# A convolution, attention and mixture block in one kernel: residual and normalisation moved ahead, attention reordered, the convolution's first column split off

## The chip, the cores and the metric

The kernel runs on one core of one Trainium2 chip. The metric is the device time of one execution in microseconds; the runs before the change had a median of 121.98 us (three runs, 121.91 to 122.46). The profile is of one execution whose own time was 122.06 us; its instructions span 120.3 us. The 1.76 us between the two lie outside the instructions.

## The reference

Eight images of 64 channels and 16 x 16 pixels, all in float32. What is computed, cut to what matters:

```python
x = x + conv_ref(ln_c(x), ...)             # ln_c: over the 64 channels, eps 1e-6
t = to_tokens(x)                           # 8 x 256 pixels, 64 channels each
t = t + ffn_ref(ln_t(t), ...)              # ln_t: over the 64 channels, eps 1e-5
...
# conv_ref
qkv = einsum('bchw,oc->bohw', x, w_qkv)    # 192 channels
dw = conv_5x5_depthwise(qkv, w_dw)
pw = einsum('bgihw,goi->bgohw', dw, w_pw)  # 24 groups of 8
ms = concatenate([qkv, pw], axis=1)        # 16 heads of 3 x 8
k, q = relu(k), relu(q); v = concatenate([v, 1])
kv = einsum('bhnd,bhne->bhde', k, v)
out = einsum('bhnd,bhde->bhne', q, kv)
out = out[..., :-1] / (out[..., -1:] + 1e-15)
out = einsum('bchw,oc->bohw', out, w_proj)
inv = bn_gamma / sqrt(bn_var + 1e-5)
out = out * inv + (bn_beta - bn_mean * inv)
...
# ffn_ref: 8 experts, 64 -> 256 -> 64, exact gelu, top 2 by gate, softmax over the two
```

## The kernel before

Every engine's program is written out by hand, in the order in which it runs, and nothing but semaphores orders the engines among each other. An instruction that waits holds up all that stands behind it on its engine. PS is the accumulator memory: eight banks of 512 floats per partition, and which piece uses which bank is a table of numbers (`XT_BANKS`, `BACK_BANKS` and so on).

The pixels are handled in four groups of 512 (`PAIRS`, index s, 0 to 3). The stages, in order of time:

- Start (0 to 15 us). Input and weights are loaded. PE turns the pixels (L1024), DVE takes their statistics, ACT the square root (L477), DVE the reciprocal root `R1` (L646 to L651). PE makes q, k and v (`qkv`, at L996) and DVE and ACT scale them out of PS half and half (L659, L464). PE turns them by heads (`turn_heads`, L1071); ACT copies each turned bank into the convolution's input (`place_own`, L484), and DVE adds the shifted neighbours out of the same bank (`place_before`, L666). There are six such pairs, and `qp_v` counts those that DVE has finished. Where PE has nothing to do, `warm_up` runs matmuls of zeros (L996 with WARM as input): one between the two turns of tokens, six before qkv, four before the convolution.
- The convolution (15 to 31 us): 240 matmuls on 32 x 32 pieces of the array (`tap`, L1112), 160 of them for v and k, 80 for q. `conv_vk` begins with two taps of two output columns of four rows each, which wait for `qp_v` 2, then goes on behind `qp_v` 4. Meanwhile DVE masks v (`first_v`, L680), splits the first layer's weights (L676), and GpSimd computes the root of the batch norm's variance by two powers (L414, L416); DVE makes of it the scale `INV`, the offset `BIAS` and the scaled projection `WPS` (`normalisation`, L697 to L702).
- Attention (31 to 62 us). `take_conv` copies the convolution's result out (L672, L489); `turn_back` (L1081) turns k and v back to pixels, `turn_input` (L1100) turns the raw input for the residual, `turn_back_q` (L1094) turns q. `second_heads` puts the second half of the heads in place (DVE L685 and L686, ACT L504 and L505), `place_q` and `second_q` (L524, L691) do so for q. `residual` makes XB, input plus BIAS (L708), `centred_residual` its mean-free copy (L716, L717). Then each group passes through a chain between PE and the other engines: `kv` (L1178), `read_kv` on DVE (L746, L749), `qt` (L1186), `relu_qt` on ACT (L537), `num` (L996, inputs KV and LATE), `attend` on DVE (L757 to L764), `attt` (L1203), `copy_attt` on ACT (L547), `proj` (L996, inputs WPS and LATE), `centre` and `whole` on DVE (L779, L784), `square_xc` on ACT (L553), `variance` on DVE (L791), `deviation` on GpSimd (L429), `scale` and `low` on DVE (L798, L804), `xt` (L1217), `copy_xs` on ACT (L557).
- Experts (from 51 us on, woven into the attention's end). `first_layer(s, e)` is four matmuls (L996, inputs XS and W1H or W1L) into two banks, `gelu(s, e)` two activations out of them (L573), `second_layer(s, e)` eight matmuls (L1293). The first six halves have two banks, all later ones four. `gate` (L996, inputs WGS and XS) gives the logits of two groups; `read_gates`, `gaps`, `places` and `softmax` on DVE and `exponential` on GpSimd (L434) give the expert weights, which `tokens` turns (L1245, L1248). They are written out and read back spread over all partitions by transfers of SyncE's queue; `combine` on DVE weighs and adds (L874, L880).

In the rows QP and CV carry the name HEADWISE, of which they are parts, and so do X2 and XC2; QT, ATT, ATTT and the scaled input of the experts are parts of LATE.

## Time and profile before

| | |
|---|---|
| median of three runs | 121.98 us |
| profiled execution | 122.06 us |
| its span | 120.3 us |
| PE busy | 115.6 us, 96% |
| DVE busy | 78.6 us, 65% |
| ACT busy | 70.0 us, 58% |
| GpSimd busy | 33.4 us, 28% |
| TensorE clock granted | full in every slice |

PE is TensorE's matmuls and PEld its weight loads, DVE is VectorE, ACT ScalarE, POOL GpSimd, SP SyncE. A matmul's busy time begins before its predecessor's ends, since they are pipelined; what one costs is best read from the distance of the starts of two blocks. "x16" behind a row is a number of instructions; a matmul of a full float32 product counts twice, since it makes two passes, a transpose once. "[0.55 <-DVE KV L749]" says that the engine stood idle for 0.55 us before the row and what released it.

### The profile page before, as it was taken

How to read it: one execution, taken by the hardware profiler on the slowest of the kernel's cores; microseconds unless marked ns; L12 is line 12 of the kernel's file. 1: busy time of each engine (PE TensorE's matmuls, PEld its weight loads, DVE VectorE, ACT ScalarE, POOL GpSimd, SP SyncE). 2: the span in 40 equal slices, each digit the busy share in tenths (PEclk: the TensorE clock that was granted, in tenths of full speed). 3: DMA queues.
4: the chain of work that ended last, by engine and by line, in shares of the span. 5: the costliest groups of instructions: out<-in, count | busy, mean ns of one | idle time of the engine just before them, and what ended most of it. 6: DMA issues, size and time to landing. Idle time of an engine off the chain costs nothing.

```text
span 120.3 us, 3332 instructions
## 1 busy us (share of the span) xinstructions
PE 115.6 (96%) x1282; PEld 85.7 (71%) x1282; DVE 78.6 (65%) x267; ACT 70.0 (58%) x134; POOL 33.4 (28%) x51
## 2 busy tenths in 40 slices
PE   6999999999999889999999999999999999999990
PEld 5489956777888688969766876766766667666660
DVE  0489595843869989988990089977319064096972
ACT  4338799030696164578891994691963919739200
POOL 6637999991000003033340040000000000000370
PEclk9999999999999999999999999999999999999999
DMA  3679500000000000000000059911089780001001
GB/s 100 180 182 224 159 8 0 5 5 5 0 0 5 0 3 0 0 5 0 0 3 0 11 173 246 237 46 44 11 242 230 212 220 16 0 0 54 0 0 46
DMA packets 5460, 8.05 MB, mean 67 GB/s; under 512 B 1412, under 2 KB 3908, under 8 KB 5444
## 3 DMA queue, kind: packets, MB, share of 16 engines
q1 hardware_dynamic: 5344, 7.80, 25.3%
q8 instruction: 10, 0.16, 0.6%
q10 hardware_dynamic: 100, 0.03, 0.2%
q14 instruction: 6, 0.05, 0.1%
HBM read 7.24 MB, written 0.59 MB: 65 GB/s over the span
## 4 chain that ended last, share of the span: by engine, by line
PE 83%; DVE 9%; ACT 2%; issue 2%; POOL 1%; POOLq 1%; DVEq 0%
PE PS L996 36%; PE PS L1293 18%; PE PS L1112 13%; PE PS L1071 2%; DVE HEADWISE L898 2%; PE PS L1178 2%; PE PS L1081 2%; PE PS L1008 2%; PE PS L1217 1%; PE PS L1094 1%; PE PS L1203 1%; POOL XP L449 1%; PE PS L1024 1%; DVE XB L717 1%; PE PS L1248 1%
## 5 line engine op out<-in xcount | busy, mean ns | idle before, releaser
L573 ACT ACTIVATE MS<-PS,B 128x512 f32<-128x512 f32 x48 | 29.1, 690 | 7.2 <-PE PS L996 7.0
L996 PE MATMUL PS<-XS,W1H 128*128 128x512 f32 x64 | 26.6, 415 | 0.0
L996 PE MATMUL PS<-XS,W1L 128*128 128x512 f32 x64 | 25.3, 395 | 0.0
L1293 PE MATMUL PS<-MS,W 128*64 128x256 f32 x192 | 22.3, 383 | 0.0
L874 DVE SCALAR_TENSOR_TENSOR WY<-PS,B,HEADWISE 128x256 f32<-128x256 f32 x24 | 10.5, 480 | 14.8 <-PE PS L1293 14.4
L1293 PEld LDWEIGHTS PS<-MS,W 128*64 128x64 f32 x192 | 13.2, 137 | 8.5 <-ACT MS L573 1.5
L996 PEld LDWEIGHTS PS<-XS,W1H 128*128 128x128 f32 x64 | 12.0, 188 | 4.9 <-ACT MS L573 1.0
L1112 PE MATMUL PS<-HEADWISE,BANDS 32*32 32x448 f32 (+2 forms) x480 | 15.3, 564 | 0.0
L449 POOL TENSOR_TENSOR XP<-XP,WY 128x256 f32<-128x256 f32 x4 | 3.2, 808 | 41.1 <-DVE WY L924 40.8
L1112 PEld LDWEIGHTS PS<-HEADWISE,BANDS 32*32 32x32 f32 x480 | 10.3, 103 | 4.5 <-issue 1.5
L996 PEld LDWEIGHTS PS<-XS,W1L 128*128 128x128 f32 x64 | 12.1, 188 | 1.8
L429 POOL TENSOR_TENSOR SM<-SM,HALF 128x4 f32<-128x4 f32 x4 | 4.0, 1009 | 25.7 <-DVE SM L791 25.7
L880 DVE TENSOR_TENSOR XP<-XP,WY 128x256 f32<-128x256 f32 x24 | 10.1, 420 | 0.4
L573 ACT ACTIVATE HEADWISE<-PS,B 128x512 f32<-128x512 f32 x16 | 9.9, 714 | 0.0
L1293 PE MATMUL PS<-HEADWISE,W 128*64 128x256 f32 x64 | 7.6, 379 | 0.0
L489 ACT ACTIVATE HEADWISE<-PS 128x512 f32<-128x512 f32 x4 | 2.2, 594 | 8.6 <-PE PS L1112 8.6
L434 POOL TENSOR_TENSOR GAP<-EULER,GAP 128x8 f32<-128x8 f32 x2 | 3.3, 1637 | 12.0 <-DVE GAP L827 12.0
L1293 PEld LDWEIGHTS PS<-HEADWISE,W 128*64 128x64 f32 x64 | 4.6, 137 | 2.3
L547 ACT ACTIVATE LATE<-PS 128x512 f32<-128x512 f32 x4 | 2.4, 599 | 6.4 <-PE PS L1203 6.4
L996 PE MATMUL PS<-WARM 128*128 128x128 f32 x28 | 4.7, 316 | 1.0 <-POOL WARM L369 1.0
L414 POOL TENSOR_TENSOR INV<-INV,HALF 128x32 f32<-128x32 f32 x1 | 5.5, 5463 | 0.1
L416 POOL TENSOR_TENSOR INV<-INV,HALF 128x32 f32<-128x32 f32 x1 | 5.4, 5434 | 0.0
(135 smaller groups left out, 182.5 us busy)
## 6 DMA issues: line engine op xcount, KB each, us to landing
HEADWISE<-spread_dram SPq DMA_DIRECT2D x14, 256.0 KB, 5.0
W<-in_w_dram SPq DMA_DIRECT2D x3, 512.0 KB, 7.9
X<-in_x_dram SPq DMA_DIRECT2D x2, 256.0 KB, 3.2
HEADWISE<-spread_dram SPq DMA_DIRECT2D x4, 128.0 KB, 3.1
out_dram<-XP SPq DMA_DIRECT2D x4, 128.0 KB, 2.4
W<-spread_dram SPq DMA_DIRECT2D x2, 256.0 KB, 6.0
VEC<-in_vectors_dram SPq DMA_DIRECT2D x1, 132.0 KB
WQ<-in_w_qkv_dram SPq DMA_DIRECT2D x2, 48.0 KB, 3.0
```

What stands on the lines that cost most here:

```text
L414: pool.tensor_tensor(INV[:, 1, 0:C // 2], INV[:, 0, 0:C // 2], HALF[:, 0:C // 2], ALU.pow).then_inc(inv_ready, 1)
L416: pool.tensor_tensor(INV[:, 1, C // 2:C], INV[:, 0, C // 2:C], HALF[:, C // 2:C], ALU.pow).then_inc(inv_ready, 1)
L429: pool.tensor_tensor(SM[:, s, 1, :], SM[:, s, 0, :], HALF[:, 0:TILES], ALU.pow).then_inc(r2_ready, 1)
L434: pool.tensor_tensor(GAP[:, 1, tiles], EULER[:, tiles], GAP[:, 0, tiles], ALU.pow).then_inc(exp_ready, 1)
L449: pool.tensor_tensor(outs[:, s, :], outs[:, s, :], WY[:, e % 4, :], ALU.add).then_inc(added, 1)
L573: act.activation(hidden(n), PS[:, h_bank(n), :], ACT.Gelu, bias=B1[:, k:k + 1]).then_inc(gelu_done, 1)
L874: dve.scalar_tensor_tensor(out=WY[:, e % 4, :], in0=PS[:, bank, at:end], scalar=B2[:, e:e + 1], in1=WB[:, s % 2, e, :], op0=ALU.add, op1=A ...
L880: i = dve.tensor_tensor(outs[:, s, :], outs[:, s, :], WY[:, e % 4, :], ALU.add)
L898: i = dve.tensor_tensor(hidden(n), hidden(n), WH[:, e - WEIGHTED, :], ALU.mult)
L996: return pe.matmul(PS[0:parts, bank, cols[0]:cols[1]], lhsT, rhs, start=start, stop=stop)
L1112: return pe.matmul(PS[32 * c:32 * c + 32, CONV_BANKS[n][r], :].rearrange("p (t y) -> p t y", y=H)[:, :, y0:y1], BANDS[rows, DY * (2 * q + ...
L1293: i = pe.matmul(PS[C * b:C * b + C, bank, at:end], W2[:, KC * e + k, :], hidden(KC * (E * s + e) + k)[:, N * b:N * b + N], start=begins an ...
```

## The change

It has five parts.

1. The raw input is turned right after the small matmuls of the start, in place of the six warm-ups, into banks that qkv uses last. ACT copies it out into XB (`take_input`), between its square root and its share of scaling; `qkv(2)` and `qkv(3)` wait for these copies. The warm-up between the turns of tokens is gone, and three of the four before the convolution.
2. The batch norm's root is computed by ACT's square root and DVE's reciprocal with a correction step, not by GpSimd's two powers; `normalisation`, `residual` and `centred_residual` stand on DVE beside the convolution. `first_v` moves from DVE to ACT.
3. The convolution's first column starts its first tap on three of four rows when `qp_v` is 1, and the fourth at 2; a third tap of this column is taken ahead of the wait for 4.
4. The attention's pieces stand in another order on PE, ACT and DVE, with other banks; `attend` is cut into `reciprocals` and `divide`.
5. `softmax(0)` stands ahead of `variance(3)`, `copy_xs`, `gate`, `tokens(1)` and some first layers stand elsewhere.

Banks, warm-ups, GpSimd and ACT:

```diff
-        WARM_UPS, WARM_UPS_BEFORE_QKV, WARM_UPS_BEFORE_CONV, TILE_BANKS = 3, 6, 4, (7, 5)
+        WARM_UPS, WARM_UPS_BEFORE_CONV, TILE_BANKS = 3, 1, (7, 5)
...
-        XT_BANKS = (6, 2)
+        XT_BANKS = (4, 5)
...
-        BACK_BANKS, BACK_Q_BANKS = (0, 1, 5, 7), (3, 4, 5, 2)
+        BACK_BANKS, BACK_Q_BANKS = (7, 0, 5, 4), (3, 1, 2, 3)
...
-            pool.wait_ge(vec_in, 16)
-            pool.tensor_scalar(INV[:, 0, :], VEC[:, 3 * C:4 * C], BN_EPS, None, ALU.add).then_inc(bn_guarded, 1)
...
-            pool.tensor_tensor(INV[:, 1, 0:C // 2], INV[:, 0, 0:C // 2], HALF[:, 0:C // 2], ALU.pow).then_inc(inv_ready, 1)
...
+            def take_input(k):
+                act.wait_ge(xt_ready, k + 1)
+                act.activation(XB[:, 0, :, :].rearrange("p (h t) c -> p t h c", h=2)[:, 4 * k:4 * k + 4],
+                               PS[:, XT_BANKS[k], :].rearrange("p (t h c) -> p t h c", t=4, h=2), ACT.Copy).then_inc(xb_copied, 1)
...
             act.activation(DEV1[:, :], VAR1[:, 3, :], ACT.Sqrt, bias=EPS1[:, :]).then_inc(dev1_ready, 1)
+            take_input(0)
+            take_input(1)
             act.wait_ge(r1_ready, 1)
...
+
+            def first_v(s):
+                for b in range(2):
+                    to, of, mask = masked_v(s, b)
+                    act.activation(to, of, ACT.Copy, scale=mask).then_inc(v_first, 1)
...
             act.wait_ge(scaled_v, 8)
             act.wait_ge(scaled_s, 8)
+            act.wait_ge(vec_in, 16)
+            act.activation(INV[:, 1, :], VEC[:, 3 * C:4 * C], ACT.Sqrt, bias=EPS2[:, :]).then_inc(inv_ready, 1)
             for s in range(PAIRS):
                 first_k(s)
             split_high()
+            for s in range(PAIRS):
+                first_v(s)
             take_conv(0)
             take_conv(1)
-            second_heads(2)
...
             act.wait_ge(b1_in, 16)
+            second_heads(1)
+            place_q(0)
+            place_q(1)
             relu_qt(0)
             relu_qt(1)
+            place_q(2)
+            place_q(3)
             copy_attt(0)
+            copy_attt(1)
+            square_xc(0)
             relu_qt(2)
+            second_heads(3)
+            square_xc(1)
             relu_qt(3)
-            square_xc(0)
-            copy_attt(1)
-            copy_attt(2)
-            square_xc(1)
             copy_xs(0)
             gelu(0, 0)
+            copy_attt(2)
+            copy_xs(1)
+            gelu(0, 1)
             square_xc(2)
             copy_attt(3)
-            gelu(0, 1)
-            copy_xs(1)
             gelu(0, 2)
+            gelu(0, 3)
+            gelu(0, 4)
```

DVE, the normalisation and its order:

```diff
+                var = VEC[:, 3 * C:4 * C]
+                link(dve.reciprocal(INV[:, 2, :], INV[:, 1, :]))
+                link(dve.scalar_tensor_tensor(out=INV[:, 3, :], in0=var, scalar=BN_EPS, in1=INV[:, 2, :],
+                                              op0=ALU.add, op1=ALU.mult))
+                link(dve.scalar_tensor_tensor(out=INV[:, 4, :], in0=INV[:, 3, :], scalar=-0.5, in1=INV[:, 2, :],
+                                              op0=ALU.mult, op1=ALU.mult))
+                link(dve.scalar_tensor_tensor(out=INV[:, 3, :], in0=INV[:, 4, :], scalar=1.5, in1=INV[:, 2, :],
+                                              op0=ALU.add, op1=ALU.mult))
+                link(dve.tensor_tensor(INV[:, 0, :], INV[:, 3, :], VEC[:, 0:C], ALU.mult))
+                dve.tensor_tensor(BIAS[:, :], VEC[:, 2 * C:3 * C], INV[:, 0, :], ALU.mult)
                 link(dve.tensor_tensor(WPS[:, 0, :], WP[:, :], INV[:, 0, :], ALU.mult))
...
+                dve.wait_ge(xb_copied, 2)
+                dve.tensor_tensor(XB[:, 0, :, :], XB[:, 0, :, :], BIAS[:, :].unsqueeze(1).broadcast_to([128, 16, C]), ALU.add)\
+                    .then_inc(xb_ready, 1)
```

```diff
             dve.wait_ge(scaled_s, 8)
-            for s in range(PAIRS):
-                first_v(s)
+            normalisation()
+            residual()
             dve.wait_ge(w_high, 2)
             split_low(0)
             split_low(1)
             dve.tensor_tensor(WGS[:, 1, :], WG[:, :], WGS[:, 0, :].bitcast(F32), ALU.subtract).then_inc(w_low, 1)
             take_conv(0)
-            normalisation()
+            centred_residual()
             take_conv(1)
-            second_heads(0)
-            residual()
 
             def read_kv(s):
...
+            second_heads(0)
             second_q(0)
+            second_heads(2)
             second_q(1)
             read_kv(0)
+            read_kv(1)
+            reciprocals(0)
+            divide(0)
             second_q(2)
             second_q(3)
-            centred_residual()
-            read_kv(1)
-            attend(0)
-            read_kv(2)
-            attend(1)
+            reciprocals(1)
+            divide(1)
+            dve.wait_ge(xb_ready, 2)
             centre(0)
             whole(0)
             variance(0)
-            attend(2)
-            read_kv(3)
+            read_kv(2)
+            centre(1)
             scale(0)
             low(0)
-            centre(1)
+            reciprocals(2)
+            variance(1)
+            divide(2)
+            read_kv(3)
+            scale(1)
             whole(1)
-            attend(3)
-            variance(1)
+            low(1)
+            reciprocals(3)
+            divide(3)
+            whole(2)
             centre(2)
-            whole(2)
-            scale(1)
-            low(1)
+            read_gates(0)
             variance(2)
-            centre(3)
-            whole(3)
+            gaps(0)
             scale(2)
             low(2)
-            read_gates(0)
-            gaps(0)
-            variance(3)
+            whole(3)
+            centre(3)
             places(0)
             softmax(0)
+            variance(3)
             scale(3)
             low(3)
-            dve.wait_ge(b2_in, 32)
             read_gates(1)
             gaps(1)
             places(1)
```

PE:

```diff
             centre_weights()
             rs()
-            warm_up(WARM_UPS_BEFORE_QKV, TILE_BANKS[1])
+            turn_input()
             pe.wait_ge(wqc_copied, 1)
             pe.wait_ge(stats_done, 2)
             qkv(0)
             qkv(1)
             pe.wait_ge(rs_copied, 1)
+            pe.wait_ge(xb_copied, 1)
             qkv(2)
+            pe.wait_ge(xb_copied, 2)
             qkv(3)
 
...
+            def turn_back(s):
+                if s == 0:
+                    pe.wait_ge(cv_v, 2)
+                    pe.wait_ge(cv_s, 2)
+                if BACK_BANKS[s] == CONV_BANKS[1][3]:
+                    pe.wait_ge(cv_s, 4)
...
                 pe.wait_ge(band_p, 4)
+                pe.wait_ge(qp_v, 1)
+                for r in range(3):
+                    tap(0, r, 0, 2, 0, *taps[0], True, False)
                 pe.wait_ge(qp_v, 2)
-                for m in (0, 1):
-                    for c in (0, 1):
-                        for r in range(4):
-                            tap(0, r, c, 2, c, *taps[m], m == 0, False)
+                tap(0, 3, 0, 2, 0, *taps[0], True, False)
+                for c, m in ((1, 0), (0, 1), (1, 1), (0, 2)):
+                    for r in range(4):
...
                         for r in range(4):
                             tap(0, r, c, 1, c - 2, *taps[m], m == 0, False)
...
-
             def kv(s):
                 pe.wait_ge(k_first, PAIRS)
                 pe.wait_ge(v_first, 2 * PAIRS)
                 pe.wait_ge(ones_set, 1)
-                if s == 0:
-                    pe.wait_ge(second_by_v, 1)
+                if s in (0, 2):
+                    pe.wait_ge(second_by_v, s // 2 + 1)
```

PE's order of the attention and the experts:

```diff
 
+            turn_back(0)
+            turn_back(1)
+            turn_back(2)
+            turn_back_q(0)
+            turn_back_q(1)
             kv(0)
-            pe.wait_ge(second_by_s, 2)
             qt(0)
             kv(1)
-            pe.wait_ge(xb_ready, 2)
             qt(1)
             num(0)
-            kv(2)
+            turn_back_q(2)
+            turn_back_q(3)
+            turn_back(3)
             num(1)
             attt(0)
+            kv(2)
+            proj(0)
+            attt(1)
             qt(2)
+            proj(1)
+            num(2)
             qt(3)
-            proj(0)
-            num(2)
-            attt(1)
+            xt(0)
             kv(3)
-            proj(1)
+            first_layer(0, 0)
             attt(2)
             num(3)
-            xt(0)
+            first_layer(0, 1)
+            xt(1)
             proj(2)
-            first_layer(0, 0)
+            gate(0)
             attt(3)
-            first_layer(0, 1)
+            first_layer(0, 2)
+            first_layer(0, 3)
             proj(3)
-            xt(1)
-            first_layer(0, 2)
-            gate(0)
-            first_layer(0, 3)
-            xt(2)
             first_layer(0, 4)
             first_layer(0, 5)
+            xt(2)
             first_layer(0, 6)
             for e in range(QUAD):
                 second_layer(0, e)
             tokens(0)
-            xt(3)
             first_layer(0, 7)
             first_layer(1, 0)
+            xt(3)
+            first_layer(1, 1)
             gate(1)
-            for e in range(1, QUAD):
-                first_layer(1, e)
+            first_layer(1, 2)
+            tokens(1)
+            first_layer(1, 3)
+            first_layer(1, 4)
             for e in range(QUAD, E):
                 second_layer(0, e)
-            tokens(1)
```

The places as they stand in the queues. First PE's queue from the statistics to the convolution, before; WARM is the input of the warm-ups, `WQC,XP` is qkv, `IDT,MSQ` the turning by heads, `HEADWISE,BANDS` the taps:

```order
L1040 MATMUL PS<-WD,SEL 32x30 x32
L996 MATMUL PS<-WARM 128x128 x6
L996 MATMUL PS<-WQC,XP 128x192 x16
L1071 MATMUL PS<-IDT,MSQ 128x128 x24
L996 MATMUL PS<-WARM 128x128 x4
L1112 MATMUL PS<-HEADWISE,BANDS 32x512 x32
```

and the same place after the change, where `IDT,X` is the turning of the raw input:

```order
L1062 MATMUL PS<-WD,SEL 32x30 x32
L1069 MATMUL PS<-IDT,X 128x128 x8
L1018 MATMUL PS<-WQC,XP 128x192 x16
L1101 MATMUL PS<-IDT,MSQ 128x128 x24
L1018 MATMUL PS<-WARM 128x128
L1135 MATMUL PS<-HEADWISE,BANDS 32x512 x16
L1135 MATMUL PS<-HEADWISE,BANDS 32x32x14 x4
L1135 MATMUL PS<-HEADWISE,BANDS 32x512 x16
```

The six warm-ups gave way to the eight transposes of the input, the four to one, and four taps of a third kind (14 lines high) stand ahead of the second half of the full ones.

PE's queue in the first part of the attention, before; `IDT,HEADWISE` is the turning back, `VM,KR` is kv, `IDT,MS` qt, `KV,LATE` num, `IDT,LATE` attt, `WPS,LATE` proj:

```order
L1081 MATMUL PS<-IDT,HEADWISE 128x4x4x8 x16
L1100 MATMUL PS<-IDT,X 128x128 x8
L1094 MATMUL PS<-IDT,HEADWISE 128x4x4x8 x16
L1178 MATMUL PS<-VM,KR 64x130 x8
L1186 MATMUL PS<-IDT,MS 128x128 x4
L1178 MATMUL PS<-VM,KR 64x130 x8
L1186 MATMUL PS<-IDT,MS 128x128 x4
L996 MATMUL PS<-KV,LATE 128x144 x4
L1178 MATMUL PS<-VM,KR 64x130 x8
L996 MATMUL PS<-KV,LATE 128x144 x4
L1203 MATMUL PS<-IDT,LATE 128x128 x4
L1186 MATMUL PS<-IDT,MS 128x128 x8
```

and after the change:

```order
L1113 MATMUL PS<-IDT,HEADWISE 128x4x4x8 x12
L1124 MATMUL PS<-IDT,HEADWISE 128x4x4x8 x8
L1199 MATMUL PS<-VM,KR 64x130 x8
L1207 MATMUL PS<-IDT,MS 128x128 x4
L1199 MATMUL PS<-VM,KR 64x130 x8
L1207 MATMUL PS<-IDT,MS 128x128 x4
L1018 MATMUL PS<-KV,LATE 128x144 x4
L1124 MATMUL PS<-IDT,HEADWISE 128x4x4x8 x8
L1113 MATMUL PS<-IDT,HEADWISE 128x4x4x8 x4
L1018 MATMUL PS<-KV,LATE 128x144 x4
L1224 MATMUL PS<-IDT,LATE 128x128 x4
L1199 MATMUL PS<-VM,KR 64x130 x8
```

Twenty transposes stand ahead of the first kv where forty stood; twelve of the others now lie between the first two nums, where one kv lay.

DVE's queue where the first two groups' projections come back (`DEN` belongs to the reciprocals, `LATE<-PS,DEN` to the division, `HEADWISE<-PS,XB` to centre and whole, `SM<-SQ` is the variance, `LATE<-HEADWISE,SM` scale and low), before:

```order
L764 TENSOR_TENSOR LATE<-PS,DEN 128x256 x2
L779 TENSOR_TENSOR HEADWISE<-PS,XB 128x256
L784 TENSOR_TENSOR HEADWISE<-PS,XB 128x2x2x64
L791 TENSOR_REDUCE SM<-SQ 128x4
L757 TENSOR_SCALAR DEN<-PS 128x64
L759 RECIPROCAL DEN<-DEN 128x64
L764 TENSOR_TENSOR LATE<-PS,DEN 128x256 x2
L746 TENSOR_TENSOR KV<-PS,CST 64x2x64 x2
L749 TENSOR_TENSOR KV<-PS,CST 128x2x16
L798 TENSOR_TENSOR LATE<-HEADWISE,SM 128x4x64
```

and after the change:

```order
L779 TENSOR_TENSOR LATE<-PS,DEN 128x256 x2
L794 TENSOR_TENSOR HEADWISE<-PS,XB 128x256
L800 TENSOR_TENSOR HEADWISE<-PS,XB 128x2x2x64
L807 TENSOR_REDUCE SM<-SQ 128x4
L756 TENSOR_TENSOR KV<-PS,CST 64x2x64 x2
L759 TENSOR_TENSOR KV<-PS,CST 128x2x16
L794 TENSOR_TENSOR HEADWISE<-PS,XB 128x256
L814 TENSOR_TENSOR LATE<-HEADWISE,SM 128x4x64
L820 SCALAR_TENSOR_TENSOR LATE<-HEADWISE,SM,LATE 128x64 x4
L769 TENSOR_SCALAR DEN<-PS 128x64
```

The reading of group 2's KV (L756, L759) now stands behind group 0's variance; before, it stood ahead of group 1's division.

## Rows read from the trace of the kernel before

**Rows 1.** The page: busy time of each engine, and the clock by slices.

```profile
PE 115.6 (96%) x1282; PEld 85.7 (71%) x1282; DVE 78.6 (65%) x267; ACT 70.0 (58%) x134; POOL 33.4 (28%) x51
PEclk9999999999999999999999999999999999999999
```

**Rows 2.** PE by stretches of the span: the stretch, its length, busy time, granted clock.

```profile
11.40:14.20 2.80, 2.80 (x27) 1.00 0.84 217
...
30.60:35.05 4.45, 4.45 (x41) 1.00 0.00 0
35.05:65.65 30.60, 29.64 (x242) 1.00 0.01 2
65.65:109.70 44.05, 44.05 (x282) 1.00 0.46 118
```

**Rows 3.** The chain that ended last: start, length, what.

```profile
46.56 1.04 PE PS L1178 x16
...
62.05 3.60 PE PS L1293 x32
...
106.64 3.01 PE PS L996 x12
...
117.78 0.43 DVE XP L937
```

**Rows 4.** Timeline of the start: start, length, engine, line, what.

```profile
4.51 0.93 PE L1024 MATMUL PS<-IDT,XP 128*128 128x128 f32 x4
...
7.05 1.60 PE L996 MATMUL PS<-WARM 128*128 128x128 f32 x12
...
9.62 2.62 ACT L464 ACTIVATE MSQ<-PS,R 128x192 f32<-128x192 f32 x8 [1.10 <-PE PS L996]
```

**Rows 5.** Timeline around the convolution, all engines.

```profile
13.71 4.04 DVE L666 SCALAR_TENSOR_TENSOR HEADWISE<-PS,CST,HEADWISE 128x512 f32<-128x512 f32 x6 [1.38 <-issue]
...
15.26 15.35 PE L1112 MATMUL PS<-HEADWISE,BANDS 32*32 32x512 f32 x480
...
16.48 0.18 PEld L1112 LDWEIGHTS PS<-HEADWISE,BANDS 32*32 32x32 f32 x16 [0.18 <-DVE HEADWISE L666]
...
25.94 1.09 ACT L489 ACTIVATE HEADWISE<-PS 128x512 f32<-128x512 f32 x2 [4.90 <-PE PS L1112]
```

**Rows 6.** Timeline of PE's queue in the attention.

```profile
32.34 1.04 PE L1100 MATMUL PS<-IDT,X 128*128 128x128 f32 x8
33.21 1.91 PE L1094 MATMUL PS<-IDT,HEADWISE 128*128 128x128 f32 x16
35.05 1.11 PE L1178 MATMUL PS<-VM,KR 128*64 128x130 f32 x16
...
40.95 1.25 PE L996 MATMUL PS<-KV,LATE 128*128 128x144 f32 x8 [0.55 <-DVE KV L749]
42.55 0.63 PE L1203 MATMUL PS<-IDT,LATE 128*128 128x128 f32 x4 [0.35 <-DVE LATE L764]
...
43.89 1.14 PE L996 MATMUL PS<-WPS,LATE 128*128 128x128 f32 x8
44.90 1.22 PE L996 MATMUL PS<-KV,LATE 128*128 128x144 f32 x8
```

**Rows 7.** Timeline of DVE, ACT and POOL in the attention.

```profile
30.59 1.29 DVE L672 COPY HEADWISE<-PS 128x512 f32<-128x512 f32 x2 [2.24 <-PE PS L1112]
31.80 0.87 DVE L685 TENSOR_SCALAR VM<-PS,CST 128x256 f32<-128x256 f32 x2
...
46.48 1.01 POOL L429 TENSOR_TENSOR SM<-SM,HALF 128x4 f32<-128x4 f32 x1 [19.00 <-DVE SM L791]
...
48.98 0.87 DVE L804 SCALAR_TENSOR_TENSOR LATE<-HEADWISE,SM,LATE 128x64 fp32r<-128x64 f32 x4
```

**Rows 8.** Timeline of ACT behind the first tokens.

```profile
66.78 0.57 ACT L557 ACTIVATE XS<-PS 128x512 fp32r<-128x512 f32 x1
67.25 1.24 ACT L573 ACTIVATE HEADWISE<-PS,B 128x512 f32<-128x512 f32 x2
```

138 lines of the change are left out of this document (58 added, 80 removed).

## The prediction

> **What bounds the kernel now.** I read the page first: PE is busy for 115.6 of 120.3 us, no other engine passes 65%, and the clock is full in every slice [rows 1]. The chain of waits then shows where the end hangs: from 46.56 us to 109.65 us nearly every piece of it is PE, and behind the last first layer (106.64) comes a tail that ends at 118.2 us with an addition on DVE [rows 3]. So time is won only if PE does less, or waits less, ahead of 109.65 us; the tail and the last store behind it (to 120.3) aren't touched. The stretches of PE say where it waits: between 65.65 and 109.70 us it is busy throughout, between 35.05 and 65.65 us for 29.64 of 30.60 us by this count [rows 2]. This count flatters, since a matmul's busy time runs on while the next one is late. I therefore took the timeline and added up the distances of the block starts in the attention: 4 transposes 0.44 (eight take 0.87), proj 1.01 (43.89 to 44.90) [rows 6], kv 1.04 [rows 3], num much the same, a first layer some 0.95 (three in 2.80 to 2.98) and 0.1 more behind another kind of block, a second layer 0.90 (four take 3.60 [rows 3]). From the first turn back (30.6) to tokens(0) (65.65) this makes 32.9 us in 35.05, so PE waits there for about 2.2 us. The two largest waits are num(1) for DVE's `read_kv` (0.55) and attt(0) for DVE's division (0.35) [rows 6]; the rest are a dozen of 0.1 to 0.3.
>
> **The start.** The eight transposes of the input cost 0.87 us (32.34 to 33.21 [rows 6]). They go where six warm-ups took 1.53 us (7.05 to 8.58 [rows 4]), so qkv can begin at 7.92 in place of 8.58 us. That by itself gives nothing: DVE and ACT scale from 9.62 us on, when `R1` is there, and need 2.62 us each [rows 4]. The cost to watch is on ACT. It is idle for 1.10 us between the square root and its scaling at 9.62 us [rows 4]. `take_input` puts two copies of 512 columns there. The nearest row has two such copies in 1.09 us [rows 5]; with the rearranged output they may take 0.1 us more. So scaling on ACT starts between 9.6 and 9.8 us; I take 9.7, a delay of 0.1 us, which `place_own`, `place_before` and the convolution inherit. qkv(2) at 9.3 and qkv(3) at 10.0 us find their banks copied at 9.1 and 9.7.
>
> **The convolution.** Before, it starts at 15.26 us, behind the second `place_before` (13.71 plus twice 0.67), does its 16 first taps in some 1.05 us, and waits for the fourth until 16.48; its 240 taps take 15.35 us, 0.064 each [rows 5]. Now three taps go at about 14.5, and 17 more between 15.3 and 16.4 us; at the fourth `place_before`, 0.1 late by ACT's copies, 20 taps are done where 16 were. The gain is 4 x 0.064 = 0.26, less 0.1: 0.16 us. At best (no delay) it is 0.26, at worst (0.2 late) 0.06. I take the end at 30.4 in place of 30.6 us, the nearest round value.
>
> **Beside the convolution.** GpSimd's two powers go, and with them nothing on the path: their result was wanted on DVE at 26.8 us, and DVE was waiting for the convolution then. On DVE the ten small operations of `normalisation` (0.26 each, an estimate from the six before) and one pass over XB's 1024 columns (1.2, at the pace of 0.6 for 512 that `take_conv` shows, two in 1.21 us from 30.59 to 31.80 [rows 7]) take the place of `first_v`; with the weights' split behind them DVE is done by 24 us, the first `take_conv` comes at 25.4. `centred_residual`, two more such passes, 2.4 us, fits between the two `take_conv`, which are some 4.9 us apart [rows 5]. On ACT `first_v` adds 8 x 0.34 = 2.7 us to a queue that is idle for 4.90 us there [rows 5]. All of this is hidden, with 1 us or more to spare; if the split came late, it would cost nothing before the first layer at 48 us.
>
> **The attention.** What goes from PE's stretch is 0.87 us of input transposes. I laid the new order out by hand with the durations above, each engine in its queue, 0.05 to 0.2 us for a handover (a matmul's result is readable some 0.2 us behind its block). The checkpoints on PE:
> - Five blocks of turning back end at 32.6 us. kv(0) needs DVE's `second_heads(0)`: `take_conv(1)` 1.2, then 1.2 for the three operations (it began at 31.80 before, its first two took 0.87 [rows 7]), so 32.9. A wait of 0.35 us; before, forty transposes covered it, and kv(0) began at 35.05 [rows 6].
> - kv, qt, kv, qt without a wait to num(0) at 35.9 (38.22 before). The other twelve transposes (1.3 us) now cover the reading of group 1 and `relu_qt(1)`: num(1) at 38.3 for 40.95, its wait of 0.55 gone. kv(2) and proj(0) cover the division of group 1: attt(1) at 41.9 for 45.96.
> - proj(1) waits for `copy_attt(1)`, 0.6 us on ACT with only qt(2) beside it: 0.35 us. num(2) waits 0.4 us for `read_kv(2)`, which stands on DVE behind variance(0) and so behind ACT's square: start at 44.5. Both waits are new.
> - xt(0) waits 0.3 us for GpSimd's power (1.01) and scale and low (0.87 [rows 7]): 46.3 for 49.94. Then first_layer(0, 0) at 47.8 for 51.25, num(3) 49.3, proj(2) 51.8, proj(3) 56.1 for 54.14 (it stands later now), first_layer(0, 6) ends at 60.5, and tokens(0) is reached at 64.1.
> The waits add up to 0.35 + 0.35 + 0.4 + 0.3 = 1.4 us where 2.2 were. The sum for this stretch: 0.87 (transposes) + 0.8 (waits) = 1.67, of which about 0.3 is lost to more changes between kinds of blocks in my layout; with 0.2 of the convolution this is 65.65 - 64.1 = 1.55 us. Ends: no wait left but the first (0.35), 3.0; all the old 2.2 back plus the new 0.35 and 0.3 of changes, 0.4. I stay with 1.55, because the layout has every queue in it.
>
> **Behind tokens(0).** `gate(1)` now stands behind first layers (0, 7), (1, 0) and (1, 1), but on ACT the copy it needs stands behind gelu(0, 7) and gelu(1, 0). From tokens(0): gelus at +1.3, +2.45, copy +3.6 to +4.2 (1.15 for two activations, 0.57 for the copy [rows 8]); PE is there at +3.9. That is 0.3 us of waiting where there was none, between 0 and 0.6. combine(0, 0) starts 1.3 us later against tokens(0), at +8.0; second_layer(0, 6), the first that needs it, is reached at +10.1, so it hides. `softmax(0)` ahead of variance(3) hides as well: the weights were there 3.4 us ahead of tokens(0). From there the order is the old one, 44 us of PE without a gap.
>
> **The sum.** 1.55 - 0.3 = 1.25; I take 1.2 us. The profiled execution's 122.06 us goes to 120.86, and since the median lies 0.08 below it, to 120.8 us.
>
> **A rule against it.** Between 30.60 and 35.05 us PE runs nothing but forty transposes, and the granted clock is full there and in all that follows; the same for 24 transposes from 11.40 to 14.20 [rows 2]. The Trainium skill ("TensorE: Matmul & The Clock Gate", the section on transposes) says that a transpose doesn't count as activity for the clock gate in the way a matmul does. By this rule the removed warm-ups, with transposes in the place of six of them, would lay the start open to a lower clock, and it would be a loss of the size of the second rival; the 4.45 us at full clock speak against it.
>
> **Rivals.**
> 1. The waits come back. If each handover costs 0.1 us more than I gave it, every block that I laid flush in the short chain between 40 and 50 us turns into a wait, since PE, DVE and ACT take turns there with one group each. The worst end of the stretch is a gain of 0.4; the middle of this case is 0.9 - 0.3 (gate) = 0.6 or less, 121.4 to 121.9 us. For it speaks that the old order had a dozen such waits, against it that the new one has a filler between most pairs. Chance 0.20.
> 2. Slower, by the clock. The place is the stretch from 11.1 to 15.3 us. Beside the transposes PE will stand idle for about 0.3 us (scaled 8), and for 0.5 between the three taps and the rest, with one warm-up in place of four. If the grant drops to the lower of its two levels (1.2 GHz), work takes twice as long: four transposes spread over 0.93 us at 4.51 [rows 4] and take 0.44 later. In the start, the low level lasted from 1.05 to about 5 us. Some 4 us of taps at half speed lose 2 us, and 1 us more if the transposes by heads are hit: 122.8 to 123.8 us. It decides only if the convolution's taps are slower than 0.1 us each. The full clock over idle times of 0.3 to 0.5 us elsewhere [rows 2, 6] speaks against it. Chance 0.07.
> 3. A larger gain. If the squares and the reading of KV come sooner than I laid them, the two new waits of 0.75 and gate's 0.3 vanish, and the gain is 1.9 to 2.3 us: 119.8 to 120.2. Chance 0.12.
> 4. The change doesn't do what it says: ACT's two copies take 0.7 us each, the column's early taps are eaten by the delay, and the middle gives only the transposes, 0.87 - 0.65 of new waits = 0.2 us. 121.8. Chance 0.05; another 0.03 for a loss that I don't see.
>
> **How the numbers follow.** My forecast has the rest, 0.53, with 120.2 to 121.4 us of its own. Half a per cent, about what a measurement of this kernel can tell from no change, is 0.61 us: faster is below 121.37, slower above 122.59. Faster: nearly all of the forecast, rival 3 and a little of rival 1, 0.68. Within: most of rival 1 and rival 4, 0.23. Slower: rival 2 and the unseen, 0.09. The range from 120.1 to 121.8 us leaves out rival 2, most of rival 3 and an edge of rival 1.
>
> **What would show it.** qkv at 7.9 to 8.0 and ACT's scaling by 9.8 us; the first tap near 14.5, a short break, and the convolution's end by 30.4 to 30.5; kv(0) at 32.9, num(1) at 38.3, attt(1) near 42; waits at proj(1) and num(2) on `copy_attt` and `read_kv`; tokens(0) at 64.1, 1.55 us sooner; a wait of 0.3 us at gate(1); the tail of 52.6 us from tokens(0) to the end longer by just that. I am wrong if tokens(0) comes later than 64.9, if taps take over 0.07 us, or if a gap opens behind 70 us.

## The result, and the profile after

The changed kernel takes 121.47 us (median of 14 runs, 121.14 to 121.88), beside 122.52 us for the kernel before on the same chip (14 runs, 121.91 to 123.15). The ratio is 0.9901, with a 95% interval from 0.9880 to 0.9923. By the ratio that is 1.2 us less (0.9 to 1.5), the forecast's size; the two medians lie 1.05 us apart. The absolute time is 0.7 us above the forecast of 120.8. Of this, 0.54 us is the base: the three runs shown first had a median of 121.98 us, all fourteen of the kernel before have 122.52.

The profiled execution took 121.62 us with a span of 119.4 us. So 2.2 us lie outside the instructions, where it was 1.76 us before. This isn't chance: it is 2.1 to 2.3 us in every run of the changed kernel and of the eleven kernels built on it below, and 1.7 to 1.8 us in every run of the kernel before and of e_late, the one kernel built on that, wherever the span is known. Some 0.5 us of what is won between the first and the last instruction is given back outside them. No run here asks by what.

The page, answering to [rows 1]: the busy time of the engines, and the clock.

```profile
PE 114.5 (96%) x1262; PEld 85.9 (72%) x1262; DVE 78.7 (66%) x265; ACT 73.4 (62%) x142; POOL 22.1 (19%) x49
PEclk9999999999999999999999999999999999999999
```

PE has 1.1 us less to do and GpSimd 11.3 us less. The page's row of the granted clock is full, as before; what it leaves out at the start is told under the experiments. Where the time went shows better in the distances between four marks that every version of the kernel has: the first `place_before` on DVE, PE's first turn back, tokens(0), tokens(2), and DVE's last addition.

| | first `place_before` | to the first turn back | to tokens(0) | to tokens(2) | to the last addition | it starts at |
|---|---|---|---|---|---|---|
| before | 13.71 | 16.82 | 35.05 | 17.84 | 34.36 | 117.78 |
| after | 13.81 | 16.83 | 33.47 | 18.42 | 34.33 | 116.86 |

So 1.58 us are won in the attention and 0.58 us lost behind tokens(0); the convolution gives nothing and the start loses 0.10 us. The last addition comes 0.92 us sooner in this pair of profiles. Over many runs the spans differ by more: a median of 119.2 us after, and of 120.4 to 120.7 us before in the four sets of runs below. The runs of the kernel before spread up to 123.15 us; none of its longer ones was profiled, so where these spend their time stays open.

The timeline of the start after the change, all engines, answers to [rows 4, 5]:

```profile
4.50 1.57 PEld L1046 LDWEIGHTS PS<-IDT,XP 128*128 128x128 f32 x8 [1.66 <-issue]
7.66 0.85 PEld L1069 LDWEIGHTS PS<-IDT,X 128*128 128x128 f32 x8
8.68 2.58 PEld L1018 LDWEIGHTS PS<-WQC,XP 64*128 64x128 f32 x32 [0.17 <-issue]
8.41 1.06 ACT L472 ACTIVATE XB<-PS 128x512 f32<-128x512 f32 x2
9.72 2.62 ACT L458 ACTIVATE MSQ<-PS,R 128x192 f32<-128x192 f32 x8 [0.24 <-PE PS L1018]
...
14.71 16.00 PE L1135 MATMUL PS<-HEADWISE,BANDS 32*32 32x512 f32 x480
```

ACT's two copies take 1.06 us and end at 9.47, before their successor's data are there, so `take_input` costs ACT nothing in this execution. But qkv begins at 8.68 us, not at 7.92: the matmuls ahead of it ran long (below), and scaling waited 0.24 us for it. The convolution now begins at 14.71 us for 15.26, and takes 16.00 us for 15.35: the early taps stretch it, and its end stays where it was, counted from the first `place_before`.

PE's weight loads in the attention, answering to [rows 6], in the new order:

```profile
30.64 1.29 PEld L1113 LDWEIGHTS PS<-IDT,HEADWISE 128*128 128x128 f32 x12 [0.73 <-issue]
33.14 0.90 PEld L1199 LDWEIGHTS PS<-VM,KR 128*64 128x64 f32 x16 [0.32 <-issue]
38.52 1.04 PEld L1018 LDWEIGHTS PS<-KV,LATE 128*128 128x128 f32 x8
42.07 0.47 PEld L1224 LDWEIGHTS PS<-IDT,LATE 128*128 128x128 f32 x4
43.47 0.97 PEld L1018 LDWEIGHTS PS<-WPS,LATE 128*128 128x128 f32 x8 [0.49 <-ACT LATE L550]
44.93 1.03 PEld L1018 LDWEIGHTS PS<-KV,LATE 128*128 128x128 f32 x8 [0.50 <-DVE KV L759]
46.71 0.42 PEld L1238 LDWEIGHTS PS<-IDT,LATE 128*128 128x128 f32 x4 [0.34 <-DVE LATE L820]
...
64.11 0.11 PEld L1266 LDWEIGHTS PS<-IDT,WDN 128*32 128x32 f32 x2 [0.38 <-issue]
```

kv(0) waits 0.32 us; num(1) (38.52) and attt(1) (42.07) start without a wait; proj(1) waits for `copy_attt`, num(2) for `read_kv`, xt(0) for `low`. The chain of waits shows what stands behind these three, answering to [rows 3]:

```profile
42.82 0.12 ACT LATE L550
...
43.31 0.42 ACT SQ L556
...
43.75 0.44 DVE SM L807
...
44.26 1.05 POOL SM L423
...
45.33 0.43 DVE LATE L814
...
46.72 0.66 PE PS L1238 x4
```

From the square of group 0 by way of variance, GpSimd's power, `scale` and `low` to xt(0), 3.4 us pass off PE, and PE has less than this to do meanwhile.

ACT behind tokens(0), answering to [rows 8]:

```profile
65.31 1.24 ACT L576 ACTIVATE HEADWISE<-PS,B 128x512 f32<-128x512 f32 x2
66.45 1.23 ACT L576 ACTIVATE MS<-PS,B 128x512 f32<-128x512 f32 x2
67.58 0.57 ACT L560 ACTIVATE XS<-PS 128x512 fp32r<-128x512 f32 x1
```

Four activations, the two gelus (0, 7) and (1, 0), stand ahead of `copy_xs(3)` (67.58), and gate(1) starts at 68.25 us, behind 0.30 us in the chain of waits that no engine fills.

### The profile page after: what moved, and what is told of

It is laid out like the page before. It is cut to its first block, busy times and chain, and to the rows that moved or that the text cites. A ratio compares the mean times of both kernels' runs of the same rounds, so it can differ in the third digit from the quotient of the medians.

```text
span 119.4 us, 3297 instructions
## 1 busy us (share of the span) xinstructions
PE 114.5 (96%) x1262; PEld 85.9 (72%) x1262; DVE 78.7 (66%) x265; ACT 73.4 (62%) x142; POOL 22.1 (19%) x49
## 4 chain that ended last, share of the span: by engine, by line
PE 87%; DVE 6%; POOL 2%; issue 2%; ACT 1%; POOLq 1%; DVEq 0%
PE PS L1018 36%; PE PS L1314 18%; PE PS L1135 13%; PE PS L1199 4%; PE PS L1101 2%; DVE HEADWISE L914 2%; PE PS L1238 2%; PE PS L1046 2%; PE PS L1113 2%; PE PS L1030 2%; PE PS L1224 2%; PE PS L1124 1%; POOL XP L443 1%; PE PS L1207 1%; POOL SM L423 1%
## 5 line engine op out<-in xcount | busy, mean ns | idle before, releaser
L890 DVE SCALAR_TENSOR_TENSOR WY<-PS,B,HEADWISE 128x256 f32<-128x256 f32 x24 | 10.5, 479 | 14.1 <-PE PS L1314 13.7
L1135 PE MATMUL PS<-HEADWISE,BANDS 32*32 32x480 f32 (+2 forms) x480 | 16.0, 564 | 0.0
L1135 PEld LDWEIGHTS PS<-HEADWISE,BANDS 32*32 32x32 f32 x480 | 12.0, 103 | 3.4 <-issue 0.4
L540 ACT ACTIVATE LATE<-PS 128x256 f32<-128x256 f32 x8 | 4.2, 622 | 2.8 <-PE PS L1207 2.8
L1018 PE MATMUL PS<-KV,LATE 128*128 128x144 f32 x32 | 4.7, 289 | 0.3 <-DVE KV L759 0.3
L411 POOL TENSOR_TENSOR BANDS<-RS,PWQ 128x320 f32<-128x320 f32 x6 | 4.6, 796 | 2.2 <-DVE R L664 2.2
L679 DVE SCALAR_TENSOR_TENSOR HEADWISE<-PS,CST,HEADWISE 128x512 f32<-128x512 f32 x6 | 4.0, 744 | 1.4 <-issue 1.4
L1018 PE MATMUL PS<-WPS,LATE 128*128 128x128 f32 x32 | 4.4, 281 | 0.2 <-ACT LATE L550 0.2
```

Of the source, the lines that this page charges most:

```text
L411: pool.tensor_tensor(*band_factors(2 - n, g), ALU.mult).then_inc(band_p, 1)
L540: i = act.activation(QT[:, s % 2, b, :].rearrange("p (y q r) -> p r q y", q=4, r=4), PS[:, CHAIN_BANK[s] + 1, :].rearrange("p (r q b y) -> ...
L679: dve.scalar_tensor_tensor(out=blocks(n, g, 1), in0=head_columns(n, g), scalar=CST[:, C_BEFORE:C_BEFORE + 1], in1=blocks(n, g, 1), op0=ALU ...
L890: dve.scalar_tensor_tensor(out=WY[:, e % 4, :], in0=PS[:, bank, at:end], scalar=B2[:, e:e + 1], in1=WB[:, s % 2, e, :], op0=ALU.add, op1=A ...
L1018: return pe.matmul(PS[0:parts, bank, cols[0]:cols[1]], lhsT, rhs, start=start, stop=stop)
L1135: return pe.matmul(PS[32 * c:32 * c + 32, CONV_BANKS[n][r], :].rearrange("p (t y) -> p t y", y=H)[:, :, y0:y1], BANDS[rows, DY * (2 * q + ...
```

## Experiments

All of them were run beside the kernel before, in four sets of runs, and medians compare best within one: e_order, e_gate, e_conv and e_warm (before at 122.26 us); e_dummy, e_late, e_var and e_order_conv (122.47); e_mean, e_soft and e_fill (122.16, on another chip than the rest); e_square (122.44). "Turn back to tokens(0)" and the like are the distances of the table above. Among kernels that are alike in the stretch they repeat to 0.1 us (33.45 to 33.55 for turn back to tokens(0) in the changed kernel, e_gate, e_conv and e_warm), so the experiments are read by these distances, of one profile each, more than by the medians.

**What carries the gain in the attention.** e_order is the changed kernel (residual, normalisation, start, convolution) with the old order and banks of attention and experts:

```diff
-            turn_back(0)
-            turn_back(1)
-            turn_back(2)
-            turn_back_q(0)
-            turn_back_q(1)
+            for s in range(PAIRS):
+                turn_back(s)
+            for s in range(PAIRS):
+                turn_back_q(s)
             kv(0)
...
             second_q(0)
-            second_heads(2)
             second_q(1)
             read_kv(0)
+            second_q(2)
+            second_q(3)
             read_kv(1)
             reciprocals(0)
             divide(0)
-            second_q(2)
-            second_q(3)
...
```

The first piece is PE's, the second DVE's; the rest of the attention and the experts follows in the old order too.

> The changed kernel with the attention's and the experts' old order on PE, ACT and DVE and the old banks, but with the residual, the normalisation, first_v and the start as changed: the transposes of the input are gone from the attention, all sixteen turns of q stand ahead of kv(0). Theory A, my sum: the removal gives 0.87 us, less what the waits take back; kv(0) begins at 34.2, tokens(0) is reached near 64.8 to 65.0, and the stretch behind it is the old 17.85, so 0.7 us faster than before, ratio 0.994. Rival 1, the order gave all and the removal nothing (PE then waits for DVE at each handover): tokens(0) at 65.4 or later, ratio 0.998 to 1.000. Rival 2, the removal gave all: tokens(0) at 64.1 to 64.3, ratio 0.988.

Measured: 120.78 us, ratio 0.9870 (0.9834 to 0.9906), turn back to tokens(0) 33.22 us, tokens(0) to tokens(2) 17.83 us. Better than the full change at both places, and its six runs (120.29 to 121.04 us) all lie below the fourteen of the change (121.14 to 121.88). My theory of 0.7 us was wrong; tokens(0) came at 63.89 us, ahead even of the second rival's 64.1. Its weight loads:

```profile
30.67 1.73 PEld L1108 LDWEIGHTS PS<-IDT,HEADWISE 128*128 128x128 f32 x16 [0.73 <-issue]
34.44 0.87 PEld L1194 LDWEIGHTS PS<-VM,KR 128*64 128x64 f32 x16 [0.17 <-issue]
39.76 1.03 PEld L1015 LDWEIGHTS PS<-KV,LATE 128*128 128x128 f32 x8 [0.18 <-issue]
```

num(1) (39.76) follows without the wait for `read_kv` of [rows 6], although PE's order is the old one. So the new order isn't needed to remove it.

What else left this place is seen on DVE. Its timeline before, at the wait of num(1):

```profile
37.59 1.21 DVE L716 TENSOR_REDUCE XBM<-XB 128x16 f32<-128x1024 f32 x1
38.84 1.23 DVE L717 SCALAR_TENSOR_TENSOR XB<-XBM,XB 128x1024 f32<-128x1024 f32 x1
40.10 0.59 DVE L746 TENSOR_TENSOR KV<-PS,CST 64x128 f32<-64x128 f32 x2
```

The two passes of `centred_residual` run right up to `read_kv(1)`.

e_dummy is e_order with eight transposes of X, whose result nothing reads, between the two turnings back. e_mean is e_order with `centred_residual` in its old place:

```diff
                 turn_back(s)
+            pe.wait_ge(cv_v, 4)
+            for t in range(8):
+                pe.transpose(PS[:, 6, 128 * (t % 4):128 * (t % 4) + 128], X[:, 128 * t:128 * t + 128], IDT[:, :])
             for s in range(PAIRS):
...
             take_conv(0)
-            centred_residual()
             take_conv(1)
...
             second_q(3)
+            centred_residual()
             read_kv(1)
```

> e_order (old order of the attention, residual moved) with eight transposes put back on PE between the turns of v and k and the turns of q, where the input's transposes stood before; nobody reads what they write. So DVE is as free as in e_order, PE has the 0.87 us of work back. From the first turn back to tokens(0) e_order took 33.2 us, before 35.04, a difference of 1.83. Theory A: only 0.87 of this are PE's transposes, the other 0.96 are waits that came from DVE's centred_residual (2.4 us between the second_q and read_kv(1), on the chain that ended last); this kernel then takes 34.1 us for the stretch, and is 0.9 us slower than e_order, ratio to before 0.994. Rival: what went with the transposes were PE's own time and waits behind them alike, and DVE's relief gives nothing without them: 34.8 to 35.0 us, ratio 0.999.

> The old order of attention and experts with the input turned at the start and the residual added beside the convolution, as in e_order, but centred_residual (two passes, 2.4 us of VectorE) back in its old place between second_q(3) and read_kv(1). It asks whether VectorE's relief is the other part of the gain, apart from TensorE's transposes. Theory (VectorE's two passes were on the path to num(1) and num(2), additive to the transposes): from the first turn back to tokens(0) 34.2 to 34.4 us, that is 33.22 + 1.13 with the whole of it, num(1) waiting again for read_kv; median 121.7 to 121.9. Rival A (the passes hide, as the prediction had it): 33.2 and 120.8. Rival B (without the transposes in front there is less cover, so the passes cost all their 2.4 us): 35.3 or more, median 122.9.

Measured: e_dummy 121.42 us, 0.9900 (0.9863 to 0.9936), turn back to tokens(0) 33.92 us. e_mean 121.65 us, 0.9956 (0.9927 to 0.9984), 34.22 us (one of its twelve runs took 628 us and is not in the ratio). The weight loads of e_mean:

```profile
38.21 0.87 PEld L1194 LDWEIGHTS PS<-VM,KR 128*64 128x64 f32 x16
39.72 1.03 PEld L1015 LDWEIGHTS PS<-KV,LATE 128*128 128x128 f32 x8 [0.64 <-DVE KV L756]
41.29 0.42 PEld L1219 LDWEIGHTS PS<-IDT,LATE 128*128 128x128 f32 x4 [0.54 <-DVE LATE L776]
```

The two largest waits of [rows 6] are back, and nothing but DVE's two passes was put back. The transposes are worth 33.92 - 33.22 = 0.70 us and the passes 34.22 - 33.22 = 1.00. If the two add, which no run with both put back shows, they make 1.70 of the 1.83 us between before (35.05) and e_order.

e_late is the kernel before with `centred_residual` moved on DVE behind the second `attend` alone:

> The kernel before with one edit: DVE's centred_residual, two passes of 1.2 us, stands behind the second attend, ahead of centre(0), and no longer ahead of read_kv(1). Everything else as before. Theory A: num(1) no longer waits for read_kv(1) (0.55 us, and 0.35 at attt(0)), both start about 1 us sooner; but the 2.4 us now stand ahead of centre(0), whose square, root and scaling lead to the first expert layer, so that much of it comes back as a wait at xt(0); 0 to 0.5 us faster than before, ratio 0.996 to 1.000. Rival, the DVE passes cost nothing where they stood: 1.000 to 1.005, with num(1) at 40.9 as before.

Measured: 122.69 us, 1.0032 (0.9998 to 1.0066), turn back to tokens(0) 35.68 us. Its weight loads:

```profile
40.39 1.03 PEld L996 LDWEIGHTS PS<-KV,LATE 128*128 128x128 f32 x8 [0.18 <-issue]
...
47.18 0.97 PEld L996 LDWEIGHTS PS<-WPS,LATE 128*128 128x128 f32 x8 [0.93 <-ACT LATE L547]
48.72 0.42 PEld L1203 LDWEIGHTS PS<-IDT,LATE 128*128 128x128 f32 x4 [0.58 <-DVE LATE L764]
```

num(1) is 0.56 us sooner than before (40.95), and the 2.4 us of DVE work then hit the groups behind it, so that the stretch is 0.63 us longer. My theory had the first half right and hoped for a gain; the rival, that nothing moves, was wrong too. At this other place in the attention the passes cost more, not less. Beside the convolution there is room:

```profile
25.93 1.29 DVE L685 COPY HEADWISE<-PS 128x512 f32<-128x512 f32 x2 [2.05 <-PE PS L1135]
27.14 1.21 DVE L728 TENSOR_REDUCE XBM<-XB 128x16 f32<-128x1024 f32 x1
28.38 1.23 DVE L729 SCALAR_TENSOR_TENSOR XB<-XBM,XB 128x1024 f32<-128x1024 f32 x1
30.63 1.29 DVE L685 COPY HEADWISE<-PS 128x512 f32<-128x512 f32 x2 [1.02 <-PE PS L1135]
```

This is DVE's timeline after the change: the two passes end at 29.61, and the second `take_conv` still waits 1.02 us for PE.

**What the orders do.** e_gate is the changed kernel with the old order behind tokens(0) on PE (`xt(3)` first, `gate(1)` behind two first layers, tokens(1) behind the second layers) and ACT (`copy_xs(3)` first):

> The changed kernel with the old order of PE and ACT behind tokens(0): copy_xs(3) right behind read_tokens(0), gate(1) behind first_layer(1, 0), tokens(1) behind second_layer(0, 7). In the changed kernel the stretch from tokens(0) to tokens(2) took 18.43 us (64.18 to 82.61) where it took 17.85 before. Theory A: the wait ahead of gate(1) (0.47 us) and 0.1 at second_layer(0, 4) are that order's doing; with the old order the stretch is back at 17.9 and the time 0.5 us shorter than the changed kernel's, ratio 0.986. Rival: variance(3), scale(3) and low(3) now end later against tokens(0) (behind softmax(0)), so that xt(3), first in the old order, waits for them, and the gain is below 0.2 us, ratio 0.989.

Measured: 121.18 us, 0.9909 (0.9874 to 0.9944), tokens(0) to tokens(2) 18.07 us for 18.42. The new order costs 0.35 us there, between my theory (0.5) and the rival (below 0.2). The weight loads of e_gate:

```profile
64.51 0.42 PEld L1234 LDWEIGHTS PS<-IDT,LATE 128*128 128x128 f32 x4 [0.24 <-DVE LATE L816]
66.65 1.09 PEld L1014 LDWEIGHTS PS<-WGS,XS 128*128 128x128 f32 x8
```

gate(1) has no wait. What is left against the old 17.84 is mostly the wait at xt(3) for `low(3)`, which comes late because ACT squares group 3 behind gelu(0, 5). So the rival named the right wait.

The same late square is what makes softmax's place matter. e_soft puts `variance(3)` back ahead of `places(0)` and `softmax(0)`; e_square does so too and puts `square_xc(3)` ahead of `copy_xs(2)` and `gelu(0, 5)`:

```diff
# e_soft and e_square, DVE
+variance(3)
 places(0)
 softmax(0)
-variance(3)
# e_square, ACT
+square_xc(3)
 copy_xs(2)
 gelu(0, 5)
-square_xc(3)
```

> The changed kernel with variance(3) back ahead of places(0) and softmax(0). The weights are ready on VectorE some us before tokens(0) turns them, so the place of softmax does nothing on the path: median within 0.3% of the changed kernel, the stretch from the first turn back to tokens(0) 33.4 to 33.6 us. Rival (softmax's earliness is what spares a wait at tokens(0), or variance(3)'s lateness costs at gate(1)): more than 0.2 us either way in one of the two stretches.

> The changed kernel with variance(3) ahead of places(0) and softmax(0), as in e_soft, but with square_xc(3) ahead of copy_xs(2) and gelu(0, 5) on ScalarE. In e_soft the variance waits 3.60 us on VectorE for this square (61.60), softmax stands behind it, and TensorE waits 1.46 us at tokens(0). Theory (softmax's place matters only because the changed ScalarE order makes the square late): with the square in the 0.57 us in which ScalarE waits for xt(2), the variance runs at 59.5, the weights are ready near 62.9 and tokens(0) is again 33.5 us behind the first turn back, so median 121.4 to 121.6. It may be 0.2 us less, since scale(3) and low(3) come 1.5 us sooner and gate(1) needs them. Rival (softmax's place itself is what counts, by VectorE's time ahead of it): the wait at tokens(0) stays above 1 us and the median near 122.6.

Measured: e_soft 122.59 us, 1.0053 (1.0034 to 1.0072), turn back to tokens(0) 34.55 us. I had expected nothing; it costs 1.08 us in the stretch, and the gain over the kernel before is gone. The timeline of e_soft, DVE and PE's weight loads:

```profile
61.60 0.42 DVE L807 TENSOR_REDUCE SM<-SQ 128x4 f32<-128x260 f32 x1 [3.60 <-ACT SQ L556]
...
64.59 0.29 DVE L872 TENSOR_TENSOR WDN<-LATE 128x32 f32<-128x32 f32 x2
65.00 0.13 PEld L1266 LDWEIGHTS PS<-IDT,WDN 128*32 128x32 f32 x2 [1.46 <-issue]
```

DVE stands idle for 3.60 us at the variance with softmax queued behind it, so the weights are there at 64.9, and PE waits. And the same places in e_square:

```profile
59.49 0.42 DVE L807 TENSOR_REDUCE SM<-SQ 128x4 f32<-128x260 f32 x1 [1.27 <-ACT SQ L556]
...
62.48 0.29 DVE L872 TENSOR_TENSOR WDN<-LATE 128x32 f32<-128x32 f32 x2
64.15 0.11 PEld L1266 LDWEIGHTS PS<-IDT,WDN 128*32 128x32 f32 x2 [0.38 <-issue]
```

e_square: 121.47 us, 0.9930 (0.9903 to 0.9958), turn back to tokens(0) 33.47, as after. With softmax in its old place and the square in time, nothing is lost, and between e_soft and e_square nothing but the square's place differs. Its hoped 0.2 us more did not come: gate(1) waits for `copy_xs(3)`, whose place on ACT is unchanged, and tokens(0) to tokens(2) stays at 18.40.

e_var is the changed kernel with `read_kv(2)` ahead of `variance(0)` on DVE:

> The changed kernel with read_kv(2) ahead of variance(0) on DVE. In the changed kernel num(2) waits for read_kv(2) until 44.93, and xt(0) starts at 46.72, behind variance, GpSimd's power, scale and low. Theory A: read_kv(2) runs in the gap ahead of the square (43.13 to 43.75), num(2) starts at 44.7, since relu_qt(2) is then the last, but variance(0) is 0.1 later and the chain through it sets xt(0): no gain, ratio 0.990 to 0.992. Rival: num(2) is the wait that counts, and all behind it comes 0.2 us sooner: 0.988.

Measured: 121.69 us, 0.9922 (0.9894 to 0.9951), 33.55 us. The weight loads:

```profile
44.74 1.03 PEld L1018 LDWEIGHTS PS<-KV,LATE 128*128 128x128 f32 x8 [0.33 <-issue]
...
46.76 0.42 PEld L1238 LDWEIGHTS PS<-IDT,LATE 128*128 128x128 f32 x4 [0.57 <-DVE LATE L820]
```

num(2)'s wait shrinks by 0.17 us and xt(0)'s grows by 0.23, and the stretch stays as it was (33.47 before this edit): the chain from the square to xt(0) is what bounds here.

**The convolution and the start.** e_conv is the changed kernel with the old order of the first taps (both columns behind `qp_v` 2, 16 taps), e_order_conv the same on e_order, and e_warm the changed kernel with the warm-up between the two turns of tokens restored:

> The changed kernel with the convolution's old order (16 taps behind the second place_before, no early column). Theory A, the early column gives what I forecast, 4 x 0.064 = 0.26 us: the convolution ends at 30.9 for 30.64, and the time is 0.25 us longer, ratio 0.992. Theory B, it gives nothing, since taps of the same rows queue behind one another and the rows' queues aren't empty when the fourth place_before comes: the end stays at 30.6 to 30.7, ratio 0.990. In the changed kernel the convolution ended only 0.1 us later than before although scaling began 0.1 us later, which speaks for B.

> e_order with the convolution's old order too, so that of the whole change only the start and the moved residual are left. In six profiles the time from the first place_before to the first turn back was 16.82 to 16.84 with the early column and 16.82 and 16.85 with the old order. Theory: the column gives nothing, ratio the same as e_order's within 0.003 (0.985 to 0.990). Rival: it gives 0.2 us, then 0.989 or more.

> The changed kernel with the one warm-up put back between the two turns of tokens. In the changed kernel the eight turns of tokens stand 0.2 us apart (4.51 to 6.05) where the last four stood 0.11 apart before, and qkv starts at 8.68, not at 7.92 as forecast. Theory A, the missing warm-up kept the clock at its lower level for longer: the second four turns are back at 0.11 us, qkv starts at about 8.1, scaling at 9.6 and not 9.72, the convolution ends 0.1 us sooner; in time 0.1 us or nothing that can be told, ratio to the kernel before 0.988 to 0.991. Rival, the clock rises at another moment in every execution whatever PE did: the turns may be slow here too, and time is the same, 0.990. Second rival, the lower clock costs more than the profile shows: 0.3 us or more faster, 0.987.

Measured: e_conv 121.55 us, 0.9928 (0.9902 to 0.9954); e_order_conv 120.58, 0.9848 (0.9802 to 0.9894), beside e_order's 0.9870; e_warm 121.38, 0.9922 (0.9896 to 0.9947). From the first `place_before` to the first turn back: 16.84, 16.84 and 16.83 us. The early column is worth nothing. The weight loads of e_conv show part of why:

```profile
14.77 0.21 PEld L1135 LDWEIGHTS PS<-HEADWISE,BANDS 32*32 32x32 f32 x16 [0.85 <-POOL BANDS L411]
15.23 0.18 PEld L1135 LDWEIGHTS PS<-HEADWISE,BANDS 32*32 32x32 f32 x8 [0.25 <-issue]
15.65 0.18 PEld L1135 LDWEIGHTS PS<-HEADWISE,BANDS 32*32 32x32 f32 x8 [0.25 <-issue]
16.02 0.18 PEld L1135 LDWEIGHTS PS<-HEADWISE,BANDS 32*32 32x32 f32 x16 [0.18 <-DVE HEADWISE L679]
```

With two columns at work, a group of four taps (eight loads) follows the one before it by 0.42 us, not by the 4 x 0.064 = 0.26 us of the full mix. What is taken ahead of the fourth `place_before` runs at this worse rate. And from the first tap behind the fourth `place_before` to the first turn back it takes 14.06 us in e_conv, with 224 taps to go (16.02 to 30.08), and 14.04 us after the change, with 220 (16.60 to 30.64). Four taps fewer in the first column save nothing there. What both orders have alike is that the third and fourth column begin only here, with all their 60 taps each; that these set the end fits the numbers, but no run shows it by itself.

As for the start, e_warm's qkv began at 8.03 us for 8.68 after the change, but e_order_conv's, without that warm-up too, at 7.95. The profiles of like starts differ among themselves: the eight turns of the tokens stand some 0.21 us apart at first and 0.11 from some moment on; in the changed kernel all eight stand at the wide distance. The traces' records of the granted clock say the same. The page counts the stretch ahead of the first record as full, but the record begins where the distance halves, so ahead of it PE ran at the lower of its two levels. With the warm-up it begins at 5.05 (e_warm), 5.13 (before) and 5.21 us (e_late). Without it, it begins at 4.02 to 5.62 us in five kernels and at 6.82 to 7.20 us in five others, the changed one (6.85) among them; e_gate's trace has no such record. So an early rise needs no warm-up between the turns. Whether the warm-up guards against the late one, three executions can't tell. The five late ones have their first `place_before` at 13.79 to 13.92 us, all others at 13.24 to 13.74. At ACT's scaling it is some 0.2 us (9.72 for 9.53 in e_warm), less than the medians can tell.

**A version of my own.** e_fill is e_order_conv with `copy_attt(3)` ahead of `square_xc(2)` on ACT and `xt(2)` ahead of `first_layer(0, 3)` on PE:

> A version of my own on e_order_conv (old attention order, old column order, residual ahead): copy_attt(3) ahead of square_xc(2) on ScalarE, and xt(2) ahead of first_layer(0, 3) on TensorE. In the profile of e_order_conv TensorE waits 0.49 us at proj(3) for copy_attt, which stood behind the square, and 0.45 us at first_layer(0, 3) for read_gates, with xt(2) ready behind it. Theory: both waits shrink, to 0.2 and 0, and 0.4 to 0.7 us is won: first turn back to tokens(0) 32.5 to 32.8 us, median 119.9 to 120.2. Rival: ScalarE's gelus, busy almost without a break from 54 to 61 us, set the second layer's start, so the wait only moves to it (0.36 us there now, 0.8 then): 33.2 and 120.6.

Measured: 121.24 us, 0.9942 (0.9920 to 0.9965), turn back to tokens(0) 33.72 us, so worse than e_order_conv's 33.19. The weight loads of e_fill:

```profile
52.23 0.97 PEld L1015 LDWEIGHTS PS<-WPS,LATE 128*128 128x128 f32 x8 [0.19 <-ACT LATE L558]
...
56.08 0.42 PEld L1230 LDWEIGHTS PS<-IDT,LATE 128*128 128x128 f32 x4 [0.46 <-DVE LATE L818]
...
59.69 0.19 PEld L1015 LDWEIGHTS PS<-XS,W1H 128*128 128x128 f32 x1 [0.59 <-issue]
```

The wait at proj(3) shrank from 0.49 to 0.19 us, as meant. But xt(2) now waits for `low(2)` itself, with a first layer behind it that could have run its first half, so ACT gets its gelu later and a new wait stands at 59.69 us. My theory was wrong; the rival had the place nearly right, but not that time would be lost by it. The best versions stay e_order_conv and e_order, which can't be told apart: the residual and the normalisation moved ahead and the start as changed, the attention and the experts in the old order. The first took 120.58 us, 1.5% below the kernel before (1.1 to 2.0).

## Why the prediction was right, and where it was not

The size of the gain, the middle and most marks came as laid out: kv(0) 33.14 for 32.9, num(1) 38.52 for 38.3, attt(1) 42.07 for 41.9, num(2) 44.93 for 44.5, xt(0) 46.71 for 46.3, tokens(0) 64.11 for 64.1 (1.47 us sooner than before for the 1.55 forecast, since this row has 65.58 before, not 65.65). The reason given for the middle was half wrong, and that the sum came out is in part luck: the attention gave 0.2 us more than laid out, while the convolution, the stretch behind tokens(0) and the time outside the instructions gave less.

- **The start.** The forecast had qkv at 7.92; 8.68 us was measured. The step that failed took PE's speed at the start as given by one profile. ACT's scaling began at 9.72 us for 9.7, but for another reason: not `take_input`, which was done at 9.47 us and cost nothing, but the wait of 0.24 us for qkv. That the number was met is luck.
- **The convolution.** The term of 0.16 us was mis-sized: it took each early tap as one tap of the full mix saved at the end, and measured 0 (16.82 us before, 16.83 after, 16.84 with the old order of taps). The end came at 30.7 us, not 30.4.
- **Beside the convolution.** Right that normalisation, residual and `first_v` hide there. Wrong in the same breath: that moving them was worth nothing. This is the step that failed. DVE had `centred_residual` between `second_q(3)` and `read_kv(1)`, right in front of the wait of 0.55 us that the prediction named as the largest. e_mean puts a price of 1.00 us on it in the old order.
- **The attention.** The forecast was 0.87 of transposes plus 0.8 of waits less 0.3, 1.37 us. The runs give 0.70 for the transposes, 1.00 for DVE's passes, 0.13 more for what else left DVE and PE there (a remainder, not measured by itself), and 0.25 against the new order: 1.58 us. The sum is nearly right, its parts are not: DVE's relief by itself takes the largest waits away in the old order, without a filler, and with it the new order costs 0.25 us where it was to win 0.5. What the fillers would have done without the relief was not run. proj(1), num(2) and xt(0) got the three waits that were forecast.
- **Softmax.** "Hides as well" was right for the kernel as it is, whose weights are ready 3.1 us ahead of tokens(0) (61.03 to 64.11). It leaves out that softmax's new place is a condition of the new ACT order: without it the gain is gone (e_soft, 34.55).
- **Behind tokens(0).** Forecast 0.3 us lost, measured 0.58. The wait at gate(1) has the forecast's 0.30 us; the loss is larger than that wait. e_gate gives back 0.35 of it; the rest fits the late square and `low(3)`, by the wait of 0.24 us at xt(3).
- **Outside the instructions.** The sum carried the time outside them over as it was (1.76 us). It is 2.2 us after the change. This term was put at nothing without a reason, and no run here shows what it is made of.
- **The rivals.** The waits did not come back beyond those forecast. The granted clock, once it had risen (at 6.85 us), did not fall again, neither over the one warm-up for four nor over the transposes from 11.5 to 14.4 us, so the second rival's loss did not come; only the rise itself was later in this profile than in that of before (5.13). The Trainium skill ("TensorE: Matmul & The Clock Gate", the section on transposes) says that a transpose doesn't count as activity for the clock gate in the way a matmul does. No drop over transposes is seen in these profiles; whether the transposes of the start put off the late rises, no run settles. The larger gain existed, but in another kernel: with the old order.

## What to carry to other kernels

Read the queue of the engine that a wait names, not only its last instruction: work that nobody is waiting for (here two passes whose result was needed 5 us later) can cost time when it stands in front of an instruction that somebody waits for: here 1.00 us for 2.4 us of work. Change one thing at a time when a reordering comes together with a relief: by the distances, the relief was worth 1.8 us here, and the reordering took 0.8 of it back (0.25 ahead of tokens(0), 0.59 behind it). And an instruction that waits for a late engine is better placed behind what is ready: `variance(3)` ahead of softmax costs 1.1 us or nothing, depending on where another engine has its square. Last, compare the span with the whole time before and after: here 0.5 us moved to where no instruction shows it.

## What the runs showed of the hardware

- Between like kernels the distance of two marks repeats to some 0.05 us in the profiles (16.82 to 16.85 for the convolution in thirteen of fourteen, 34.30 to 34.36 for the tail in all), while the median of the kernel before moves from 122.16 to 122.52 us between sets of runs. The exception was e_fill, with 17.15 us in the convolution.
- The moment at which PE's granted clock rises to its upper level differs by execution: 4.02 to 7.20 us from the start in the ten records of kernels without the warm-up between the turns, 5.05 to 5.21 in the three with it. The page's clock row doesn't show it; the distance of the transposes does (0.21 against 0.11 us).
- Taps of 32 x 32 pieces run four in 0.26 us in the full mix, and four in 0.42 us when only two columns of the array are served. With 220 or 224 taps left when the last two columns begin, the rest takes the same 14.0 to 14.1 us.
- The time outside the instructions is 1.7 to 1.8 us in the kernel before and in e_late, and 2.1 to 2.3 us in the twelve kernels with the changed start and normalisation.
